# One tile for attention's queries and the convolutions' first batch, a reciprocal root in steps, and feed-forward set-up inside the second convolution

## What is computed

```
B, H, W, C = (16, 56, 56, 64);  NH = 8;  KD = C // NH;  FF = 256;  EPS = 1e-06
x = x + _dwconv(x, pos_w, pos_b)                          # 3 x 3
y = _layernorm(x, ln1_g, ln1_b)
q = y @ q_w + q_b;  k = (y @ k_w + k_b) * SCALE;  v = y @ v_w + v_b
lepe = _dwconv(v, lepe_w, lepe_b)                         # 5 x 5
attn_w = softmax(einsum('bhqnd,bhknd->bhnqk', qh, kh) + mask_w)
vw     = einsum('bhnqk,bhknd->bhnqd', attn_w, vh)
attn_h = softmax(einsum('bqwnd,bkwnd->bwnqk', qh, kh) + mask_h)
out    = einsum('bwnqk,bknwd->bqwnd', attn_h, vw)
x = x + (out.reshape(b, h, w, NH * KD) + lepe) @ out_w + out_b
y = _layernorm(x, ln2_g, ln2_b)
x = x + gelu(y @ fc1_w + fc1_b) @ fc2_w + fc2_b
# _layernorm: (x - m) * rsqrt(v + EPS) * g + b over the 64 channels
```

## Time and profile before

| | us |
|---|---|
| median of 3 runs (2100.58, 2105.39, 2103.77) | 2103.77 |
| the profiled execution | 2106.22 |
| its span in the trace | 2104.4 |
| `pos` up to attention's first instruction | about 318 |
| attention | 318 to about 1565 |
| `lepe` | 1565 to about 1787 |
| `mlp` | 1787 to the end |

### The profile page before, as it was taken

The page is one execution under the profiler, slowest core; times in us unless marked ns, Lnnn a source line. Parts: engine busy times, 40 slices in busy tenths (PEclk is TensorE's granted clock), DMA queues, the critical chain, the costliest instruction groups (busy, mean ns, idle before and its releaser), DMA issues. The chain is left out here.

```text
span 2104.4 us, 89182 instructions
## 1 busy us (share of the span) xinstructions
PE 1852.3 (88%) x34510; PEld 1548.6 (74%) x34510; DVE 1428.2 (68%) x2270; ACT 1247.0 (59%) x2107; POOL 1173.6 (56%) x1858
## 2 busy tenths in 40 slices
PE   5877624999999999999999999999978995599998
PEld 5877522888887888877887877878768995477776
DVE  3588864777776777766777766767642663688885
ACT  4677734555555555564555555555544766488887
POOL 6477855554555554454555554555534001599997
PEclk8888755999999999999999999999988998799999
DMA  9589566678787787778787787776748994466663
GB/s 141 99 197 223 160 190 148 158 172 180 177 178 167 176 178 177 161 179 186 182 186 175 177 186 172 181 185 161 184 89 148 201 233 142 111 137 137 137 137 82
DMA packets 661152, 346.82 MB, mean 165 GB/s; under 512 B 562462, under 2 KB 613406, under 8 KB 660878
## 3 DMA queue, kind: packets, MB, share of 16 engines
q1 hardware_dynamic: 627782, 298.69, 65.1%
q0 software_dynamic: 31936, 43.83, 7.0%
q10 hardware_dynamic: 1160, 0.13, 0.1%
HBM read 105.42 MB, written 102.76 MB: 99 GB/s over the span
## 5 line engine op out<-in xcount | busy, mean ns | idle before, releaser
L813 ACT ACTIVATE att_prob<-att_st_ps 128x448 f32<-128x448 f32 x896 | 486.9, 544 | 439.0 <-PE att_st_ps L720 438.9
L888 DVE TENSOR_REDUCE att_mm<-att_s_ps 128x8 bf16<-128x448 f32 x896 | 556.2, 621 | 266.9 <-PE att_s_ps L690 263.2
L733 PEld LDWEIGHTS att_pv_ps<-att_vx,att_prob 128*56 128x56 f32 x14336 | 562.0, 132 | 89.2 <-issue 5.6
L733 PE MATMUL att_pv_ps<-att_vx,att_prob 128*56 128x18 f32 x14336 | 514.4, 202 | 5.8 <-ACT att_prob L813 4.3
L582 POOL DMA_DIRECT2D att_mvt<-att_mneg x256 | 136.3, 537 | 555.3 <-ACT att_mneg L802 484.9
L690 PE MATMUL att_s_ps<-att_kx,att_q_unit 120*56 120x448 bf16 x1792 | 347.2, 360 | 9.1 <-DMA att_q_unit<-att_qk_hi 7.4
L715 PE MATMUL att_st_ps<-att_mvt,set_both 122*56 122x448 bf16 x1792 | 345.7, 357 | 9.6 <-DMA att_mvt<-att_mneg 8.3
L720 PE MATMUL att_st_ps<-att_qx,att_k_hi 128*56 128x448 bf16 x1792 | 344.4, 356 | 0.0
L720 PE MATMUL att_st_ps<-att_qx,att_k_lo 128*56 128x448 bf16 x1792 | 342.1, 353 | 0.0
L573 POOL DMA_DIRECT2D att_qx<-att_q_hilo x512 | 245.8, 488 | 2.0 <-issue 1.7
L796 ACT ACTIVATE att_qk_hi<-att_pj,set_bias 128x392 bf16<-128x392 f32 x256 | 150.2, 587 | 124.9 <-PE att_pj L648 124.7
(11 more groups left out here) (209 smaller groups left out, 3196.4 us busy)
## 6 DMA issues: line engine op xcount, KB each, us to landing
att_xt<-xn_chunks SPq DMA_DIRECT2D x128, 196.0 KB, 3.4
att_k_hi<-att_qk_hi SPq DMA_DIRECT2D x128, 196.0 KB, 3.5
att_k_lo<-att_qk_lo SPq DMA_DIRECT2D x128, 196.0 KB, 3.8
att_qx<-att_q_hilo POOLq DMA_DIRECT2D x512, 49.0 KB
pos_x<-in_x_dram SPq DMA_DIRECT2D x128, 105.0 KB
lepe_x<-v_scratch SPq DMA_DIRECT2D x128, 105.0 KB, 4.2
x_scratch<-pos_x SPq DMA_DIRECT2D x128, 98.0 KB
xn_chunks<-pos_xrt SPq DMA_DIRECT2D x16, 784.0 KB, 5.2
```

The costliest lines, as they stand in the source:

```text
L733: ins = pe.matmul(pv_ps[v % 2][64 * h:64 * h + L, at:at + 18], prob[t % 4][:, 4 * h + a, :], vx[v][:, VW * j + 36 * a + 18 * h:VW * j + 36 ...
L813: act.activation(out, src, ACT.Exp).then_inc(exp_done, 1)
L888: dve.tensor_reduce(mm[v % 2][:, NH * j:NH * j + NH], s_ps[j % 2][:, 0:S8].rearrange("p (s k) -> p s k", k=L), AX.X, ALU.max).then_inc(max ...
```

## The change

1. **A shared tile.** `FirstTile` is allocated once for the whole kernel (128 x 15360 bf16, the size of X[0]). It is X[0] in both convolution phases and `qx[0]` in attention. When attention's last column image has finished with `qx[0]` (chunk 1's last transposed scores) and its chunk-3 values are built, GpSimd clears the whole tile (7680 f32 on each partition), after it has issued the maxima of chunk 3. SP waits for that and then loads images 0 and 1 of the values in the body of chunk 2, and image 2 in that of chunk 3; `lepe` starts with a load of image 3 only. In `lepe` the two engines that cleared X[0] now clear X[1] instead, GpSimd's later memset of X[1] is gone, and the memsets of the three `add` tiles move from GpSimd to DVE.
2. **The inverse deviation of `pos`.** GpSimd's power is replaced by a square root on ACT (`root(n)`, after the second of the four convolved copies of iteration n), a reciprocal on DVE (`flip(n)`, at the end of iteration n), and on GpSimd one Newton step in five small operations (`inverse(n)`). `mlp` keeps its power.
3. **Feed-forward set-up.** `MlpSetup` owns the parameters and their splitting. Its tiles and semaphores outlive `lepe`. Its sixteen DMAs go out on SP in `lepe` at image 7, its DVE steps at the ends of iterations 0 and 9 to 15. `mlp` no longer makes an identity, loads the attention rows first, and its TensorE start waits only for four memsets of x1 and four of PSUM; ACT waits for the bias (`biased`).

```diff
+class FirstTile:
+    def __init__(self, al):
+        self.tile = al.sb("first", [128, PITCH], BF16)
+        self.images = self.tile[:, :].bitcast(F32).rearrange("p (n s j c) -> p n s j c", n=4, s=2, c=C)
+        self.queries = self.tile[:, 0:NH * UW].rearrange("p (s t) -> p s t", s=NH)
+        self.clear, self.x_in = al.sem("first_clear"), al.sem("first_in")
...
@@ attention_phase, sync body
                 elif is_there(*n6):
                     load_x(*n6)
+                if i.known and not i.rows and i.at == B - 1 and v >= 2:
+                    if v == 2:
+                        sp.wait_ge(first_tile.clear, 1)
+                        load_image(sp, first_tile.images, v_d, 0, 0, first_tile.x_in)
+                    load_image(sp, first_tile.images, v_d, 0, v - 1, first_tile.x_in)
...
@@ attention_phase, gpsimd body
+                if i.known and not i.rows and i.at == B - 1 and v == 2:
+                    pool.wait_ge(st_done, cnt(i, 1, 7, 7))
+                    pool.wait_ge(vx_done, cnt(i, 3, 4, 4))
+                    pool.memset(first_tile.tile[:, :].bitcast(F32), 0.0).then_inc(first_tile.clear, 1)
...
@@ conv_phase, sync
             for b in range(2):
-                sp.wait_ge(framed[b], FRAME_PARTS[b])
-                for q in range(NB4):
+                if pos or b:
+                    sp.wait_ge(framed[b], FRAME_PARTS[b])
+                for q in range(0 if pos or b else 3, NB4):
                     load(b, q)
...
+                    if n == 7:
+                        mlp.parameters(sp)
...
@@ conv_phase, gpsimd
-                    pool.wait_ge(var_in, n + 1)
-                    pool.tensor_scalar(st[u][:, 1, :], st[u][:, 1, :], EPS, None, ALU.add).then_inc(eps_done, 1)
-                    pool.wait_ge(eps_done, n + 1)
-                    pool.tensor_tensor(st[u][:, 2, :], st[u][:, 1, :], half[:, :], ALU.pow).then_inc(rs_done, 1)
+                    inverse(n)
...
+                pool.wait_ge(sd_done, n + 1)
+                pool.tensor_scalar(var, var, EPS, -0.5, ALU.add, ALU.mult).then_inc(eps_done, 1)
+                pool.wait_ge(eps_done, n + 1)
+                pool.wait_ge(flipped, n + 1)
+                pool.tensor_tensor(r, var, r0, ALU.mult).then_inc(newton, 1)
+                pool.wait_ge(newton, 3 * n + 1)
+                pool.tensor_tensor(r, r, r0, ALU.mult).then_inc(newton, 1)
+                pool.wait_ge(newton, 3 * n + 2)
+                pool.tensor_scalar(r, r, 1.5, None, ALU.add).then_inc(newton, 1)
+                pool.wait_ge(newton, 3 * n + 3)
+                pool.tensor_tensor(r, r, r0, ALU.mult).then_inc(rs_done, 1)
...
@@ conv_phase, scalar
+                act.wait_ge(var_in, n + 1)
+                if n >= 2:
+                    act.wait_ge(xn_done, n - 1)
+                act.activation(st[u][:, 2, :], st[u][:, 1, :], ACT.Sqrt, bias=eps[:, 0:1]).then_inc(sd_done, 1)
...
@@ conv_phase, vector
+            def flip(n):
+                dve.wait_ge(sd_done, n + 1)
+                if n >= 2:
+                    dve.wait_ge(rs_done, n - 1)
+                dve.reciprocal(st[n % 2][:, 3, :], st[n % 2][:, 2, :]).then_inc(flipped, 1)
...
+                    flip(n)
...
+                    mlp.weights(dve, n)
...
@@ mlp_phase, vector
             for t in x1[0:4]:
-                done(dve.memset(t[32:64, :, :].rearrange("p j c -> p (j c)"), 0.0))
+                dve.memset(t[32:64, :, :].rearrange("p j c -> p (j c)"), 0.0).then_inc(cleared, 1)
             for t in (*o_ps[0:2], *y_ps):
-                done(dve.memset(t[:, :], 0.0))
-            settled()
-            dve.sem_inc(gaps, 1)
-            dve.wait_ge(par, 16 * 16)
...
+                dve.memset(t[:, :], 0.0).then_inc(cleared, 1)
+            dve.wait_ge(cleared, 8)
+            dve.sem_inc(ready, 1)
             dve.wait_ge(pre_pe, 1)
```

281 lines of the change are left out of this document (166 added, 115 removed).

## The result

| | before | changed |
|---|---|---|
| median of the runs, us | 2103.81 (2100.58 to 2105.39) | 2080.55 (2078.17 to 2086.41) |
| profiled execution, us | 2106.22 | 2079.97 |
| its span | 2104.4 | 2078.1 |

The ratio is 0.9896, with a 95% interval of 0.9872 to 0.9919. The changed kernel was run once more beside some of the experiments and gave 0.9857 (0.9828 to 0.9886). As points these are 22 and 30 us; the intervals overlap between 0.9872 and 0.9886. The forecast of 23 lies inside the first interval and just outside the second, which begins at 24.

What follows compares the result with a forecast made beforehand. GpSimd's path bounds the loop of `pos` (14.6 us per image, beside SP's DMA loop of 14.7), data the starts of `lepe` and `mlp`. -14 + 11 - 10.4 + 0.3 - 10.1 = -23.2 from 2103.8 gives 2081; range 2073 to 2091.

Steps and rivals of the forecast that it cites:

- Part 1: Loop of `pos`: replacing GpSimd's addition and power by root, reciprocal and Newton step saves 14 us.
- the bounds of -6 and -19: Loop of `pos`: -6 if only the shorter last wait and part of the switch's slack count, -19 if centering doesn't suffer.
- the gain is 4 + 5 = 9: `pos` up to batch 3's relays: copies of batch 1 end 4 us earlier, plus 5 of slack at the relay.
- from then on the loop saves nothing with relays: `pos` behind batch 3's first relay: images with relays keep a period near 13.6 us, as before.
- the sum of 15: `pos`: 9 up to batch 3's relays, 3 in four images without relays, 3.3 at the last scaling; taken as -14.
- Part 2: Attention's end: clearing and 24 early loads delay the last stores, which the barrier awaits; +11 us, bounds +7 and +14.
- Part 3: Start of `lepe`: first convolution at 18.4 instead of 27.1 us and at full speed; -10.4, bounds -8 and -12.
- Part 4: Feed-forward set-up: +0.3 us in `lepe`; first `front` of `mlp` at 6.0 in place of 16.1, -10.1.
- Gains little: Loop of `pos`: DMAs and SP's 14.7 us loop bind, so -6 in place of -14, 2089; chance 0.17.
- More comes back: Centering in `pos` doesn't suffer from relays, or attention's stores end earlier: 4 to 5 us more, 2076; chance 0.22.
- The loads don't help: Attention's end and `lepe`: memset and loads come too late, +8 instead of +0.6 together, 2088; chance 0.04.
- Slower: Loop of `pos`: DVE's reciprocal waits for ACT's root, closing a longer loop; above 2105; chance 0.03.

Runs made afterwards that it cites:

- e1: Changed kernel with GpSimd's addition of epsilon and power back in `pos`, without root, reciprocal and Newton step; ratio to before 0.9957.
- e8: Changed kernel with SP's 24 early loads moved behind attention's last four stores, still ahead of the barrier; ratio to before 0.9871.
- e9: Changed kernel with one more 784 KB store by SP for each of images 0 to 4 of `pos`; ratio to before 0.9895.
- e4: Changed kernel with the shared tile cleared in four parts and only images 0 and 1 loaded at attention's end; ratio to before 0.9828, median 2068.28.
- e5: Changed kernel with only image 0 loaded at attention's end, behind the undivided memset; ratio to before 0.9816, median 2064.59.

## Why the prediction was right

The forecast was 2081 and the median 2080.55. That is better than its terms deserve, and in part luck: one of them was too small, and scatter of the executions and of the medians hid it. Outside attention's own stretch the changed kernel's two traces are 28.1 and 29.5 under the one of before, against the 23.2 of the sum. In the first comparison attention's own stretch took 1.8 back, and the medians lie 3.0 closer together than the two profiled executions. The second median of the changed kernel, 2073.89, is 7 below the forecast, still inside its range of 2073 to 2091.

- **Part 1, the loop of `pos`: -14 forecast, -18.5 measured** (e1), just inside the bounds of -6 and -19. Up to batch 3's relays the path was right and so was the sum, "the gain is 4 + 5 = 9" against 9.1 (189.39 to 180.29), or 7.7 from e1 (187.99): the relays now wait for the DMA, as the forecast had it. Its two terms were off in opposite ways, and that they cancelled was luck. The issue of batch 3's last load ended at 176.90 in place of 179.53, 2.6 earlier and not 4 (1.6 against e1's 178.51), and the relay follows it by 3.4 in place of 9.9, so 6.5 of slack went and not 5. The terms that failed for the sum stand behind that point. Between e1 and the changed kernel I compare the scalings from image 7 on. The four images with relays took 57.35 against 53.80: 3.6 gained, where the forecast said "from then on the loop saves nothing with relays". The next three took 38.14 against 34.67, 1.16 each where it said 0.7. The last took 12.72 against 9.15, 3.6 for a forecast 3.3. And of the sum of 15 one was struck off "for waits not followed here".
- **Why the images with relays gained.** The centering does suffer from relays that are under way, as I took it, though it reads one large tile and 28 broadcast values and not two large tiles (2.35 to 3.92 us at six images of the changed kernel, 2.02 to 2.03 at the ten others). But I gave it 1.6 more at every image, 5.6 for centering and scaling together. Behind the switch VectorE waited for no more than one relay: it came in between the two, the second relay then took 2.8 in place of 1.0, and centering and scaling took 4.8 to 5.2 together. The period was 12.7, not 13.6; about half of that is this, the rest the next point. The rows, with the two relays merged into one (1.0 and 2.8), and VectorE's centering:

```profile
205.56 3.81 POOL L1209 COPY pos_xg<-pos_x 128x480 f32<-128x480 f32 x2
206.11 2.36 DVE L1598 SCALAR_TENSOR_TENSOR pos_xc<-pos_st,mlp_first 128x1792 f32<-128x1792 f32 x1
```

- **Why the images without relays gained more.** I added durations: 4.0 + 2.02 + 2.02 + 3.7 + 0.3 = 12.0. The starts of successive operations on VectorE lie up to 0.1 closer than the durations say (a scaling started 1.94 behind a centering of 2.02). Scaling to scaling is 11.56.
- **Part 2, attention's end: +11 forecast, +11.1 measured.** 24 loads and four stores between 1534.42 and 1550.87 are 16.5; the forecast's sum was 16.3 (1554.3 to 1570.6). e8 shows that the reason was the right one of the two: the time of issue. By the forecast's own sum a landing as before gives 9.9 (1570.6 + 2.1 against 1562.8), not the 9 that it names for that case.
- **Part 3, `lepe`: -10.4 forecast.** The first convolution came at 18.9, not 18.4, in place of 27.5 by the same row (the forecast's 27.1 is the product just ahead of it), and at 1.93: 8.5 + 1.7 = 10.2. The phase as a whole shrank by 9.5: TensorE's wait for the last batch grew from 6.5 to 8.6, for a reason that is open. The set-up in it cost nothing in place of 0.3.
- **Part 4, `mlp`: -10.1 forecast, -9.1 to -9.4 measured.** The `front` came at 6.7, not 6.0: the loads of x1 were issued from 1770.49, 2.0 after the start as forecast, and with their landing they took 0.7 longer than I gave them. The phase as a whole shrank by 8.0, as from the `front` on it took 302.9 in place of 301.5.
- **The rivals.** "Gains little" is out: the DMAs do bind up to the switch, as its argument had it (e9), but the relays behind the switch came 9 us earlier all the same. "More comes back" is out for attention's end; for `pos` it named the right size (4 to 5 more), though the wrong mechanism, since the centering did suffer. Its bound of -19, "the centering does not suffer", is nearly reached for other reasons. "The loads don't help" at +8 is out: parts 2 and 3 together lie between +1.6 and -4.0, around the forecast's +0.6. "Slower" is out: the reciprocal waited at most 1.55 for ACT's root, at the second image, and not in the loop shown above.

## What to carry to other kernels

A transfer that is hidden in a phase's last microseconds has to be hidden with its issue: here 24 loads cost SP 13 us ahead of a barrier, as much as they saved behind it. Loading only as many as fit ahead of the last result kept the gain for 2 us of tail with 16 loads (e4); with 8 (e5) the phase behind was 2.4 longer. Where an engine's step is replaced by a shorter one, follow the loop until its next owner: here part of the stretch belonged to the DMAs, and the gain came at the switch and behind it. To compare edits of a few microseconds in a long kernel, subtract the stretch that none of them touches.
